# Windowed attention in blocks of 32 queries and 64 keys, eight heads to a step, in place of 96 queries and 128 keys, four heads to a step

## The reference

```python
q, k, v = heads(x @ Wqkv)
q = rotary(l2norm(q) * qs); k = rotary(l2norm(k) * ksc)
# block of 32 queries against its own 32 keys and the 32 before; each query sees the last 33
mask = (it < jb) | (it > jb + 32) | (jb == -1)
sim = where(mask, -max, einsum('bhwie,bhwje->bhwij', q, k2) * 8.0)
out = einsum('bhwij,bhwje->bhwie', softmax(sim), v2) @ Wo
```

## Time and profile before

| | |
|---|---|
| three runs | 6245.43, 6246.88 and 6255.48 us, median 6246.88 |
| profiled execution, span from first to last instruction | 6252.3 us |
| PE, PEld busy | 5488.2 us (88%), 3026.7 us (48%) |
| DVE, ACT, POOL busy | 4222.1 us (68%), 3746.9 us (60%), 2596.2 us (42%) |
| the network's first product on PE | 1857.19 us after the start |
| DMAs that move Q and K | 3072, 64.0 KB each, 2.0 us from issue to landing |

### The profile page before, as it was taken

The page is one execution under the profiler, slowest core; times in us unless marked ns, Lnnn a source line. Parts: engine busy times, 40 slices in busy tenths (PEclk is TensorE's granted clock), DMA queues, the critical chain, the costliest instruction groups (busy, mean ns, idle before and its releaser), DMA issues. The chain is left out here.

```text
span 6252.3 us, 104394 instructions
## 1 busy us (share of the span) xinstructions
PE 5488.2 (88%) x31072; PEld 3026.7 (48%) x31072; DVE 4222.1 (68%) x6918; ACT 3746.9 (60%) x11805; POOL 2596.2 (42%) x2014
## 2 busy tenths in 40 slices
PE   7888887777768999899999999899998999899997
PEld 3333333222225555555555555555555555555553
DVE  5677766333337777777777777777777777777775
ACT  3444444223226777677766777677766677667775
POOL 1122212000005555555555555455555555555552
PEclk9999998777779999999999999999999999999998
DMA  1000000000012222222222222222222222222222
GB/s 40 0 0 0 0 0 21 0 0 0 0 53 52 48 50 54 52 52 49 49 57 52 49 50 50 53 55 51 48 55 51 53 48 48 55 55 48 50 50 65
DMA packets 160228, 244.68 MB, mean 39 GB/s; under 512 B 51280, under 2 KB 51280, under 8 KB 158928
## 3 DMA queue, kind: packets, MB, share of 16 engines
q1 hardware_dynamic: 159696, 238.34, 15.5%
HBM read 30.52 MB, written 6.29 MB: 6 GB/s over the span
## 5 line engine op out<-in xcount | busy, mean ns | idle before, releaser
L323 POOL TENSOR_TENSOR c_Pb<-c_Pb,c_rs 96x512 f32<-96x512 f32 (+1 forms) x960 | 996.5, 1038 | 1385.6 <-DVE c_rs L717 1385.6
L385 ACT ACTIVATE c_Pb<-c_S,c_nb 96x128 f32<-96x128 f32 (+1 forms) x3840 | 1345.2, 360 | 107.2 <-DVE c_nb L708 105.8
L724 DVE COPY c_PTs<-c_S 128x384 f32<-128x384 f32 (+1 forms) x960 | 557.8, 581 | 608.2 <-PE c_S L506 607.7
L708 DVE TENSOR_REDUCE c_nb<-c_S 96x4 f32<-96x512 f32 (+1 forms) x960 | 657.4, 685 | 391.2 <-PE c_S L496 390.9
L335 POOL TENSOR_TENSOR c_rot<-c_tAB 128x1024 f32<-128x1024 f32 x384 | 908.6, 2366 | 0.0
L396 ACT ACTIVATE c_OT<-c_PO 128x192 f32<-128x192 f32 (+1 forms) x960 | 323.6, 337 | 762.6 <-PE c_PO L520 762.1
L385 ACT ACTIVATION_READ_ACCUMULATOR c_Pb<-c_S,c_nb 96x1 f32 (+1 forms) x3840 | 763.4, 199 | 0.0
L329 POOL TENSOR_TENSOR c_sqs<-c_sq 128x512 f32<-128x512 f32 x384 | 487.8, 1270 | 612.8 <-ACT c_sq L363 612.8
L496 PE MATMUL c_S<-c_QK 64*96 64x128 f32 (+1 forms) x7680 | 665.2, 292 | 0.0
L506 PEld LDWEIGHTS c_S<-c,c_Pb 96*128 96x128 f32 (+1 forms) x3840 | 427.0, 141 | 368.7 <-issue 209.3
L520 PE MATMUL c_PO<-c_PTs,c_V 128*64 128x96 f32 (+1 forms) x7680 | 554.8, 266 | 20.0 <-issue 19.4
(11 more groups left out here) (267 smaller groups left out, 10828.2 us busy)
## 6 DMA issues: line engine op xcount, KB each, us to landing
c_QK<-c_F SPq DMA_DIRECT2D x3072, 64.0 KB, 2.0
c_stage<-in_w_heads SPq DMA_DIRECT2D x36, 256.0 KB, 2.9
a_W<-in_w_level SPq DMA_DIRECT2D x1, 3335.5 KB, 10.8
c_WT<-in_w_tails SPq DMA_DIRECT2D x6, 537.5 KB, 5.2
b_W<-in_w_level SPq DMA_DIRECT2D x1, 3133.0 KB, 10.2
c_WT<-in_w_tails SPq DMA_DIRECT2D x6, 512.0 KB, 4.2
x<-in_x SPq DMA_DIRECT2D x1, 2048.0 KB, 7.7
x_kept<-x SPq DMA_DIRECT2D x1, 2048.0 KB, 6.3
```

Of the source, the lines that this page charges most:

```text
L323: nc.gpsimd.tensor_tensor(p, p, r, ALU.mult).then_inc(*p_ready.up())
L385: e = nc.scalar.activation(Pb[0:m, n % 3, i, :], S[0:m, 2 * (n % 2) + r, c * SPAN_K:(c + 1) * SPAN_K], ACT.Exp, bias=nb[0:m, n % 2, i:i + ...
L708: nc.vector.tensor_reduce(nb[0:m, n % 2].rearrange("p (b c) -> p b c", b=2), S[0:m, b:b + 2, 0:2 * SPAN_K].rearrange("p b (c k) -> p b c k ...
L724: nc.vector.tensor_copy(PTs[:, n % 2].rearrange("p (b c) q -> p b c q", b=2)[:, :, :, 0:m], S[:, b:b + 2, 2 * SPAN_K:].rearrange("p b (c q ...
```

## The change

- **Shapes.** A step takes 8 heads (a side) and 128 queries, as four blocks of 32 queries with 64 keys each. A turn has `NS = 8` steps in place of 20. For each head and block there is one score product of 64 rows, 32 weight columns and 64 moving columns (32 in a step, 64 records) and one value product of 64 rows, 64 weight columns and 32 moving columns (32 in a step, 64 records). Four transposes take two heads each.
- **Banks.** The transposes overwrite the first bank of the step's slot in `S`, the value products of both heads of a pair its second; `PO` goes, and `PD` takes the sums of squares. `scores(n)` waits for `out_copy(n - 2)`.
- **Lag.** `turn_probs`, `values` and `pt_copy` lag by one step; `inv_sum(n)` and `normalise(n)` stand in step n itself. `PTs` has one buffer.
- **Projections.** One Q/K job in each step (`both`), its `finish` a step later. The tables are no longer multiplied ahead: `products` has the scale as a third operand. V is projected in eight units of four fp32 products (256 moving columns, 64 weight columns) straight from `xf`, all copied by DVE into `VO`; four more DMAs in every second step lay the other alignment into `VE` (`shift_values`). V's weights aren't split, so `divide` has four pieces in place of six.

```diff
-LOOK = 32
-SPAN_K = 128
-SPAN_Q = SPAN_K - LOOK
+WIN = 32
+KEYS = 2 * WIN
+WINDOWS = SEQ // WIN
...
...
+SIDES = 2
+HS = HEADS // SIDES
+PS = HS // 2
+NS = SIDES * TILES
+JOBS = 8
...
-        S = ctx.enter_context(nc.psum_tensor("c_S", [P, 4, 512], F32))
-        PO = ctx.enter_context(nc.psum_tensor("c_PO", [P, 512], F32))
...
+        S = ctx.enter_context(nc.psum_tensor("c_S", [P, 2, 2, 512], F32))
...
+        PD = ctx.enter_context(nc.psum_tensor("c_PD", [P, 512], F32))
...
+        def job(n, now, nxt):
+            return (n - 2) % NS, nxt if n >= 2 else now
+        def job_before(n, now, nxt):
+            return (n - 3) % NS, nxt if n >= 3 else now
+        def v_unit(n, now, nxt):
...
+            return (n + 3) % NS, nxt if n >= 5 else now
...
+                def shift_values(side, part, turn):
+                    v = 4 * side + 2 * part
+                    sp.wait_ge(*v_put.nth(v + 2, turn))
+                    lo, hi = (0, 3) if part == 0 else (3, 7)
+                    for r in range(2):
+                        a, b = slice(64 * r, 64 * r + WIN), slice(64 * r + WIN, 64 * r + KEYS)
+                        sp.dma_start(VE[a, side, lo:hi, :], VO[b, side, lo:hi, :]).then_inc(ve_in[2 * side + part].sem, 16)
+                        sp.dma_start(VE[b, side, lo:hi, :], VO[a, side, lo + 1:hi + 1, :]).then_inc(ve_in[2 * side + part].sem, 16)
...
-                    p = Pb[0:m, n % 3]
-                    r = rs[0:m, n % 2, :].unsqueeze(2).broadcast_to([m, 4, SPAN_K])
-                    nc.gpsimd.tensor_tensor(p, p, r, ALU.mult).then_inc(*p_ready.up())
+                    p = Pb[:, n % 2]
+                    nc.gpsimd.tensor_tensor(p, p, rs[:, n % 2, :].unsqueeze(2).broadcast_to([P, HS, KEYS]), ALU.mult).then_inc(*p_ready.up())
...
+                    j, tj = job(n, now, nxt)
+                    if tj:
+                        add_squares(j, tj)
+                    if now:
+                        normalise(n, now)
+                    if tj:
+                        rotate(j, tj)
...
-                    for i in range(4):
-                        r, c = i // 2, i % 2
-                        e = nc.scalar.activation(Pb[0:m, n % 3, i, :], S[0:m, 2 * (n % 2) + r, c * SPAN_K:(c + 1) * SPAN_K], ACT.Exp,
-                                                 bias=nb[0:m, n % 2, i:i + 1], scale=1.0, accum_out=sums[0:m, n % 2, i:i + 1])
+                    for i in range(HS):
+                        c, r = i // 2, i % 2
+                        e = nc.scalar.activation(Pb[:, n % 2, i, :], S[:, n % 2, r, c * KEYS:(c + 1) * KEYS], ACT.Exp,
+                                                 bias=nb[:, n % 2, r * PS + c:r * PS + c + 1], scale=1.0, accum_out=sums[:, n % 2, i:i + 1])
...
+                    j, tj = job(n, now, nxt)
+                    jb, tb = job_before(n, now, nxt)
+                    m, tm = back(n, 1, now, prev)
+                    if prev and n == 3:
                         norm_squares(prev)
-                    if prev and n == 7:
+                    if prev and n in (4, 5):
+                        gate_copy({4: 0, 5: 2}[n], prev)
+                    if tb:
+                        inverse_norm(jb, tb)
+                    if tj:
+                        square(j, 0, tj)
+                        square(j, 1, tj)
+                    if prev and n == 3:
                         norm_root(prev)
...
+                    if now:
+                        exp(n, now)
+                    if prev and n == 4:
+                        gate_copy(1, prev)
                     if tm:
                         out_copy(m, tm)
...
+                    if prev and n == 5:
                         gates(prev)
...
+                def both(j, turn):
+                    if j == 0:
+                        pe.wait_ge(*shifted.nth(2, turn))
+                    if turn.seq == 0 and j % 2 == 0:
+                        pe.wait_ge(*split.nth(j + 2, Turn(turn.layer, 0, 1)))
+                    if j or not turn.first:
+                        pe.wait_ge(*prods.nth(2 * j, turn))
+                    proj(j, 0, turn, PA)
+                    if turn.first and 3 < j < 7:
+                        pe.wait_ge(*v_put.nth(j - 3, turn))
+                    elif not turn.first or j == 7:
+                        pe.wait_ge(*v_put.nth((j - 3) if j > 3 else (j + 5) - NS, turn))
+                    proj(j, 1, turn, PB)
...
+                    if j or not turn.first:
+                        pe.wait_ge(*finished.nth(j, turn))
+                    nc.tensor.matmul(PD[:, :], ones_head, sq[:, 0], start=True, stop=True).then_inc(*summed.up())
...
+                    for a in range(2):
+                        for r in range(2):
+                            mm = nc.tensor.matmul(PB[64 * r:64 * r + 64, a * VR:(a + 1) * VR], xf[:, at + KEYS * a:at + KEYS * a + KEYS],
+                                                  WV[:, side, r * VR:(r + 1) * VR], start=True, stop=True)
...
+                        nc.tensor.matmul(S[:, n % 2, r, 0:PS * KEYS], const.identb, const.mask[i > 0], start=True, stop=False, skip_group_check=True)
+                    for c in range(PS):
+                        for b in range(4):
+                            q0, k0 = i * TILE + WIN * b, keys(4 * i + b)
+                            for r in range(2):
+                                rows = slice(64 * r, 64 * r + 64)
+                                mm = nc.tensor.matmul(S[WIN * b:WIN * b + WIN, n % 2, r, c * KEYS:(c + 1) * KEYS], QK[rows, side, 0, c, q0:q0 + WIN],
+                                                      QK[rows, side, 1, c, k0:k0 + KEYS], start=False, stop=c == PS - 1, skip_group_check=True)
...
+                    for c in range(PS):
+                        mm = nc.tensor.transpose(S[:, n % 2, 0, c * TILE:(c + 1) * TILE],
+                                                 Pb[:, n % 2, 2 * c:2 * c + 2, :].rearrange("p r k -> p (r k)"), ident)
...
+                    pe.nop(nofuse=True)
+                    for c in range(PS):
+                        for b in range(4):
+                            v, k = window(4 * i + b)
+                            for r in range(2):
+                                rows = slice(64 * r, 64 * r + 64)
+                                mm = nc.tensor.matmul(S[rows, n % 2, 1, c * TILE + WIN * b:c * TILE + WIN * b + WIN],
+                                                      v[rows, side, k, c * DH:(c + 1) * DH], PTs[rows, c, WIN * b:WIN * b + WIN], start=True, stop=True)
...
+                    j, tj = job(n, now, nxt)
+                    v, tv = v_unit(n, now, nxt)
+                    m, tm = back(n, 1, now, prev)
+                    if tj:
+                        both(j, tj)
                     if now:
                         scores(n, now)
                     if tm:
+                        turn_probs(m, tm)
+                    if prev:
+                        if n == 0:
+                            out_proj(0, prev)
+                        if n == 1:
+                            out_proj(3, prev)
+                        if n == 2:
+                            out_proj(6, prev)
+                            out_proj(7, prev)
+                        if n == 3:
+                            if tj:
+                                pe.wait_ge(*prods.nth(2 * j + 1, tj))
+                            variance(prev)
+                        if n == 4:
+                            gate(1, prev)
+                        if n == 7:
+                            value(2, prev)
+                    if tm:
                         values(m, tm)
...
+                    if prev:
+                        if n == 0:
+                            out_proj(1, prev)
+                        if n == 1:
+                            out_proj(4, prev)
+                        if n == 6:
+                            value(0, prev)
+                        if n == 7:
+                            outer(prev)
+                    if tj:
+                        sumsq(j, tj)
+                    if tv:
+                        if tj:
+                            pe.wait_ge(*prods.nth(2 * j + 2, tj))
+                        v_proj(v, tv)
+                    if prev:
+                        if n == 0:
+                            out_proj(2, prev)
+                        if n == 1:
+                            out_proj(5, prev)
                         if n == 2:
...
+                            centre(prev)
+                        if n == 3:
+                            gate(0, prev)
                             pe.wait_ge(*lnv.nth(1, prev))
...
+                        if n == 4:
+                            gate(2, prev)
+                        if n == 6:
+                            value(1, prev)
...
-                    nc.vector.tensor_tensor(tAB[:, half], bank[:, :].unsqueeze(1).broadcast_to([P, 2, SEQ]), table, ALU.mult).then_inc(*prods.up())
...
```

(35 more changed lines are left out.)

540 lines of the change are left out of this document (160 added, 380 removed).

## The result

The changed kernel takes 6371.9 us (median of 4 runs, 6365.65 to 6378.08), the kernel before 6251.2 us beside it: ratio 1.019, 95% interval 1.0177 to 1.0204. It is 1.9% slower; I had forecast 6383. The profiled execution took 6378.1 us.

A forecast was written before the change was run, and what follows sets the result against it. PE sets the pace before; after, each step's chain runs through DVE. From the profiled 6252.3 us: +221 for longer turns, -75 at weight changes, -10 at the start: 6388, median 6383 us; range 6110 to 6920.

The forecast's parts named there:

- Slower, by the chain through DVE and ACT: Each step's chain runs through DVE, so an ordinary turn takes 92.6 us against 88.0; slower at 0.68.
- Step 1: Start of a step: V's copy, 0.25 plus 0.69 us, beside the job's first half; second half 0.98 to 1.68 us.
- Step 3: Scores within a step: 64 records, two side by side, 32 x 0.053 + 0.2 = 1.9 us, ending at 3.93.
- first rival: Eight tiles side by side: scores 0.6 us, step 8.85, turn 88.3, median 6176 us; chance 0.26.
- Step 4: After the scores: DVE leads for 4.2 us, to 8.1; values take 1.85 us beside 2.5 us of DVE.
- Extras of steps 3 to 6: ACT's delays on top of 10.15 us a step: 0.6 together in steps 3 to 5, 2.1 in step 6.
- the likeliest case: Score records run in pairs, scores 1.9 us a step: 6383 us, own range 6240 to 6560; chance 0.42.
- The clock at 1.00 in ordinary turns: Sign expected in the changed kernel's profile: PE's clock stays full in ordinary turns.
- a rival with 2 to 6 us a turn: PE's gaps of 1.5 to 3 us in steps 3 to 6 lower the clock to 0.93: 6480 to 6670; chance 0.12.
- Serial values, by the bank: A pair's value products run one after the other, 3.4 us a step: turn 103.5, total 6911 us; chance 0.11.
- Records' own pace: Short records at 0.076 us each: scores 4.9, values 4.4 us, over 30 us a turn, above 7800; chance 0.05.
- Change of weights: Four divisions for six and no tables: 5 us over ordinary turns in place of 20.3, 75 us less in all.

The follow-up runs named there:

- fill56: Changed kernel plus unread bf16 products before PE's wait for the copy of the transposes, 18 in step 5 and 24 in step 6: 6269.4 us.
- act_both: Changed kernel with ACT's inverse norm before the feed-forward square or copy (steps 3 to 5), and step 5's gates before its exponentials: 6124.6 us.
- values_by_head: Changed kernel with each step's 64 value records reordered, all 32 of the even heads, then all 32 of the odd heads: 7367.9 us.

## Why the prediction was right, and where it was not

- **Slower, by the chain through DVE and ACT**: right. The array's work fell, and the turn grew since most steps wait for a chain over PE, ACT and DVE. The orders alone give back 571 us without taking any work out. That the number fits as well as it does (6371.9 against 6383) is luck, as the next points show.
- **Step 1** (copy of V, second half at 0.98): right to 0.1 us. The second half starts 0.86 us after the end of V (3182.83 to 3183.69); behind a feed-forward product the copy is hidden, and PE doesn't wait for it.
- **Step 3, the scores at 1.9 us: wrong**, 0.79 measured. The price of one record held (0.056); the step that failed is "the trace shows two side by side and never more", an absence taken for a limit. The first rival, with 0.6, was nearest: eight steps with 1.11 us less in each should have made the turn 8.9 us shorter.
- **Step 4** (4.2 us from scores to the end of DVE, values 1.85): near. Where ACT leaves it alone it is 3.8 us (step 1), and in steps 3 to 5 it is 4.9; the values take 1.84. The form with a third operand takes 1.28 us, not 1.21.
- **Extras of steps 3 to 6**: as the likeliest case had them (0.2 each), too small; as the first rival had them (1.5 in each of 3 to 5), nearly right: the first `products` start 1.1 us later there than in steps 1, 2 and 7. Of the 8.9 us, 3.8 came back, which leaves 5.1: 3.1 of them in steps 3 to 6, and 0.6 in step 0, where the first rival had `finish_turn` at 0.8.
- **"The clock at 1.00 in ordinary turns": wrong**, 0.93. This was a rival with 2 to 6 us a turn, and it cost 5.2. I had PE's gaps nearly right (1.5 to 3 us in steps 3 to 6; measured are 0.9 in step 3, 1.2 in step 4, 2.1 in step 5, 2.8 to 4 in step 6, and 2.1 in step 2) and the row that showed a lower clock beside such gaps, and took the case without it. The clock on top of the first rival, 88.3 + 2 to 6, is what happened (87.5 + 5.2); no case of mine joined the two.
- **Serial values, by the bank**: did not happen; a pair takes 0.058 us. The Trainium skill (TensorEngine Tiling, Restrictions and Gotchas, PSUM Pressure) says that different row tiles cannot access the same bank at the same time. Here the two write different partitions of it, and nothing is lost. Two row tiles on the same partitions of one bank were not tried. **Records' own pace** did not happen either: 64 scores in 0.79 us are 0.012 each. The Trainium skill (TensorE: Matmul & The Clock Gate, Step-by-step) gives about 62 ns per matmul for a sequencer that decodes in software, which is not what this trace shows.
- **Change of weights**: 3.5 us over ordinary turns (17.6 / 5) against 5 forecast, 20.4 before. **Network's start**: first product 19.1 us earlier, not 10, but the first turn as a whole later, so +8.9 in the account. The last turns (-20.7) I had not priced.

What stays open: why the clock falls in one turn of act_both and not in the next, with the same instructions; why with the fillers of fill56 it falls in step 2 more often; and how much of values_by_head's surplus is the clock alone.

## What to carry to other kernels

When PE's work shrinks and the time does not, lay one step's start times of all engines beside each other, and look for an instruction that waits for a late input while its engine's next one has had its input for microseconds (here a gate copy before an inverse norm). Exchanging the two took 154 us off here, where the cut in PE's work had taken off none. A gap of 2 us on PE costs more than its length if the clock falls behind it, so price the stretch behind the gap at both levels, and if the gap can't be closed, work that nobody reads can be the cheaper filling. A forecast whose sum comes out right has to be checked term by term: here two terms of 5 us cancelled.

## What was unexpected of the hardware

Of the score records on eight different tiles (two halves of rows, four quarters of columns) eight started within 0.05 us: 64 took 0.79 us, against 0.056 us for each where neighbours share a tile. Reordering the same records changed their time by a factor of nearly three and the kernel's time by nothing or by 3%. A wait of 2.1 us on PE was followed by 6.8 us at 1.2 GHz; all 26 ordinary turns of the changed kernel hold stretches at that level, and 42 short unread products a turn took 102 us off. A fall in step 5 alone cost 0.2 us, since ACT held up the next step anyway; what a fall costs depends on what waits behind it.
